# A graph layer's per-edge weights summed on GpSimd relation by relation, and VectorE's drain moved inside a pass

## The reference, cut to what matters

```python
N, IN, OUT, R, E = (2500, 768, 768, 8, 40000)   # called with 1250 nodes and 41250 edges, sorted by dst

def _rgcn_conv(x, src, dst, etype, W, root, b):
    seg = dst * num_rel + etype
    sums = jax.ops.segment_sum(x[src], seg, num_segments=num_nodes * num_rel)
    cnt = jax.ops.segment_sum(jnp.ones((src.shape[0],)), seg, num_segments=num_nodes * num_rel)
    mean = (sums / jnp.maximum(cnt, 1.0)[:, None]).reshape(num_nodes, num_rel, -1)
    return jnp.einsum('nri,rio->no', mean, W) + x @ root + b

h = relu(_rgcn_conv(xn, src, dst, etype, W1, root1, b1))
out = _rgcn_conv(h, src, dst, etype, W2, root2, b2)
```

## Time and profile before

| | |
|---|---|
| time, median of 3 | 3421.99 us (3419.77 to 3424.31) |
| the profiled execution | 3421.39 us, of it the span 3419.5 us |
| PE busy | 3174.5 us, 93% of the span |
| DVE busy | 1773.6 us, 52% |
| POOL busy | 1273.2 us, 37% |
| chain that ended last | PE 71%, DVE 12%, issue 7%, DVE's sequencer 6% |

### The profile page before, as it was taken

How to read it: one execution, slowest core, us unless ns; L and a number is a source line. 1 busy time by engine, 2 the same in 40 slices (tenths; PEclk the granted TensorE clock), 3 DMA queues, 4 the chain that set the end, 5 groups by cost and what they waited for, 6 DMA issues and landing times.

```text
span 3419.5 us, 64810 instructions
## 1 busy us (share of the span) xinstructions
PE 3174.5 (93%) x19556; PEld 2359.9 (69%) x19557; DVE 1773.6 (52%) x2941; ACT 762.8 (22%) x1086; POOL 1273.2 (37%) x1377
## 2 busy tenths in 40 slices
PE   6999999999997999999899989999886999999999
PEld 5788888777776888888677766776654555555555
DVE  7576666555555333333555552334586456455551
ACT  2211121000001212211000004444212543543540
POOL 2681000577772000002777761000420632652562
PEclk9999999999999999999999999999998999999999
DMA  5334334599994232321898882000330000000003
GB/s 149 101 106 149 118 116 137 171 306 307 306 306 140 87 120 94 118 95 63 319 307 307 303 287 78 14 28 14 88 95 24 20 1 19 19 1 19 19 28 95
DMA packets 101141, 433.58 MB, mean 127 GB/s; under 512 B 19648, under 2 KB 19971, under 8 KB 96818
## 3 DMA queue, kind: packets, MB, share of 16 engines
q0 software_dynamic: 55712, 266.87, 23.2%
q1 hardware_dynamic: 42593, 124.83, 11.6%
q10 hardware_dynamic: 2736, 40.50, 3.4%
HBM read 355.21 MB, written 76.88 MB: 126 GB/s over the span
## 4 chain that ended last, share of the span: by engine, by line
PE 71%; DVE 12%; issue 7%; DVEq 6%; ACT 1%; POOL 1%; DMA 1%; POOLq 0%; SPq 0%; ACTq 0%
PE PS L1466 26%; PE PS L1580 13%; PE PS L1776 5%; PE PS L1604 3%; PE PS L1711 3%; PE PS L1475 3%; DVE NM L1387 2%; PE PS L1612 2%; PE PS L1759 2%; PE PS L1760 2%; PE PS L1715 2%; PE PS L1649 2%; DVE HOT L1166 2%; PE PS L1633 2%; PE PS L1623 1%
## 5 line engine op out<-in xcount | busy, mean ns | idle before, releaser
L1466 PE MATMUL PS<-WHL,XT 128*125 (+1 forms) x3240 | 549.4, 329 | 7.0 <-DVE WHL L940 4.2
L1466 PE MATMUL PS<-WHL,HT 128*125 (+1 forms) x3240 | 531.8, 327 | 0.0
L1580 PE MATMUL PS<-GATA,HOT 128*125 128x384 f16 x2880 | 492.6, 328 | 37.0 <-issue 17.8
L1466 PEld LDWEIGHTS PS<-WHL,XT 128*125 (+1 forms) x3240 | 441.3, 138 | 92.7 <-issue 5.3
L1466 PEld LDWEIGHTS PS<-WHL,HT 128*125 (+1 forms) x3240 | 441.9, 137 | 84.2
L558 POOL DMA_INDIRECT GATA<-msg_table,SKEY x432 | 421.8, 976 | 163.0 <-issue 124.6
L1580 PEld LDWEIGHTS PS<-GATA,HOT 128*125 x2880 | 386.3, 137 | 114.5 <-issue 44.6
L1166 DVE SCALAR_TENSOR_TENSOR HOT<-NODE,DSTF,WHLO x720 | 297.0, 475 | 277.6 <-issue 277.6
L594 POOL TENSOR_TENSOR PL<-PF 125x500 bf16<-125x500 f32 (+1 forms) x360 | 320.6, 924 | 281.0 <-ACT PF L797 277.8
L1016 DVE SCALAR_TENSOR_TENSOR MSG<-PS,MSG 125x768 f16<-125x768 f32 x160 | 153.1, 957 | 360.3 <-ACT MSG L627 358.9
L627 ACT ACTIVATE MSG<-PS 125x768 f16<-125x768 f32 x160 | 129.6, 810 | 786.8 <-PE PS L1466 773.9
(11 more groups left out here) (254 smaller groups left out, 3898.6 us busy)
## 6 DMA issues: line engine op xcount, KB each, us to landing
msg_table<-MSG SPq DMA_DIRECT2D x160, 336.0 KB
WST<-in_wg_dram ACTq DMA_DIRECT2D x16, 2304.0 KB, 10.1
WST<-in_wf_dram SPq DMA_DIRECT2D x7, 1536.0 KB, 6.3
KROW<-key_rows POOLq DMA_DIRECT2D x54, 192.0 KB, 3.8
GATA<-msg_table,SKEY POOLq DMA_INDIRECT x432, 4.5
msg_table<-MSG SPq DMA_DIRECT2D x160, 39.0 KB
WST<-in_wm_dram SPq DMA_DIRECT2D x5, 1152.0 KB, 5.1
GATB<-msg_table,SKEY POOLq DMA_INDIRECT x216, 4.5
```

The lines of the kernel that those rows point to most:

```text
L1466: ins = pe.matmul(PS[0:ROWS, b0 + h, 0:HALF], X[:, xp, k, bass.ts(t, ROWS)], panel_part(slot, wp, k, h), start=k == 0 and xp + wp == 0, st ...
L1580: ins = pe.matmul(PS[0:ROWS, bass.ds(((n + (L + 1)) % 2) * 2 + h, 1), 0:HALF].rearrange("p a c -> p (a c)"), HOT[:, bass.ds((n % 2) * AT + ...
```

## The change

The weights are summed one relation at a time, as `GW` gets each column (`relation_in`), between GpSimd's key rows in layer 0 and before the gathers in layer 1, without the common factor, which `common_weight` multiplies in when all eight are known. In layer 0 the first four gathers are issued ahead of `edge_weights`, which now holds only the inverse counts and the split. In the passes the drain goes from ahead of the one-hots to the start of `take_pass`, which the final addition of a layer also calls.

```diff
+            def relation_weight(L, r):
+                g.wait_ge(S["relation_in"], L * REL + r + 1)
+                g.sem_inc(S["pool_tick"], 1)
+                if r == 0:
+                    g.tensor_scalar(WSUM[:], ETF[:, 0:TILES], 0.0, GW[:, 0:1], ALU.is_equal, ALU.mult)
+                else:
+                    g.tensor_scalar(TMPF[:], ETF[:, 0:TILES], float(r), GW[:, r:r + 1], ALU.is_equal, ALU.mult)
+                    g.drain()
+                    g.tensor_tensor(WSUM[:], WSUM[:], TMPF[:], ALU.add)
+                g.drain()
+            def common_weight(L):
                 g.wait_ge(S["relations_made"], L + 1)
                 g.sem_inc(S["pool_tick"], 1)
-                g.tensor_scalar(WSUM[:], ETF[:, 0:TILES], 0.0, GW[:, REL:REL + 1], ALU.is_equal, ALU.mult)
-                for r in range(1, REL):
-                    ... (mask times column, drain, add, drain)
+                g.tensor_scalar(WSUM[:], WSUM[:], GS[:, 1:2], None, ALU.mult)
+                g.drain()
+            def edge_weights(L):
                 (inverse counts, split, weights_made: as before)
+            for u in range(SLOTS):
+                (wait keys_made, send KROW: as before)
+                if u % RT == RT - 1:
+                    p = COUNTED + u // RT
+                    for r in range(0 if p == COUNTED else p, p + 1):
+                        relation_weight(0, r)
             for L in range(2):
-                edge_weights(L)
+                if L == 1:
+                    for r in range(REL):
+                        relation_weight(1, r)
+                common_weight(L)
+                if L == 1:
+                    edge_weights(1)
                 g.wait_ge(S["msg_out"], ROW_IN * REL * RT * (L + 1))
                 for t in range(TILES):
+                    if L == 0 and t == AT:
+                        edge_weights(0)
...
-                    v.tensor_copy(GW[:, bass.ds(p, 1)], SC[:, WINV])
+                    v.tensor_copy(GW[:, bass.ds(p, 1)], SC[:, WINV]).then_inc(S["relation_in"], 1)
...
-                    v.tensor_scalar(GW[:, REL:2 * REL], GW[:, 0:REL], GS[:, 1:2], W_TOP, ALU.mult, ALU.mult)
+                    v.tensor_scalar(GS[:, 1:2], GS[:, 1:2], W_TOP, None, ALU.mult)
...
                 def take_pass(n):
+                    v.drain()
                     v.wait_ge(S["pass_done"], n + (L + 2))
...
                         n = v.snap(cnt, min_val=0, max_val=1 << 20)
-                        v.drain()
                         v.wait_ge(S["pass_done"], n + (L + 1))
```

More of the change, by code:

```diff
@@ L148, in graph_and_attentions_kernel @@
         WHLO = sb(gctx, "WHLO", [128, TILES, 2], f16)
-        GW = sb(gctx, "GW", [128, 2 * REL], f32)
+        GW = sb(gctx, "GW", [128, REL], f32)
         GS = sb(gctx, "GS", [128, 3], f32)
@@ L213, in graph_and_attentions_kernel @@
             edges_in zeros_made bounds_made bounds_t lim_made
-            hot1_made hot1_used cnt_done hir_made hir_out key_in0 key_in1 key_in2 key_in3 key_in4 keys_ready low_made relations_made inverse_made rows2_in keys_made counts_found counts_taken
+            hot1_made hot1_used cnt_done hir_made hir_out key_in0 key_in1 key_in2 key_in3 key_in4 keys_ready low_made relations_made relation_in inverse_made rows2_in keys_made counts_found counts_taken
             hot_made gat_in0 gat_in1 gat_in2 gat_in3 gat_in4 gat_in5 gat_in6 gat_in7 gat_in8 gat_in9 gat_in10 gat_in11 pass_done pass_out group_used weights_made msg_hi rows_done
@@ L540, in edge_weights @@
                 g.sem_inc(S["weights_made"], 1)
-            for L in range(2):
-                edge_weights(L)
+            g.wait_ge(S["hir_out"], 16)
+            for u in range(SLOTS):
+                if u >= KRING:
+                    g.wait_ge(S["keys_made"], u - KRING + 1)
+                    g.sem_inc(S["pool_tick"], 1)
+                g.dma_start(KROW[:, u % KRING, :], key_rows[u:u + 1, :].broadcast_to([128, SLOT * 128])).then_inc(S[f"key_in{u % KRING}"], 16)
+                if u % RT == RT - 1:
+                    p = COUNTED + u // RT
+                    for r in range(0 if p == COUNTED else p, p + 1):
+                        relation_weight(0, r)
+            for L in range(2):
+                if L == 1:
[4 more added lines that the diff above has]
+                    edge_weights(1)
                 g.wait_ge(S["msg_out"], ROW_IN * REL * RT * (L + 1))
```

## The result

The changed kernel takes 3427.03 us (median of 20 runs, 3423.47 to 3430.99), the kernel before 3420.14 (20 runs, 3409.53 to 3429.01): a ratio of 1.0019 [1.0013, 1.0026], 6.9 us or 0.19% slower. The forecast was slower, 3434 us. The direction holds and the time lies in the range, but the size is half of what was forecast: 3434 us is 13.9 above the 3420.14 of these 20 runs. The profiled execution of after took 3427.76 us, its span is 3425.9 us; that is 6.4 us over the profiled one of before.

The account below looks back on a forecast made before the run. GpSimd's gathers were taken to bound both layers' passes before, VectorE layer 0 afterwards. 3421.4 + 10.7 (layer 0) + 1 (layer 1) = 3433.1, with the median 0.6 above the profiled execution: 3434 us, range 3424 to 3446.

Parts of the forecast that it names:

- weights and front gathers at nothing: Panels and ring start: GpSimd's waits of 24.72 us (layer 0) and 27.53 us (layer 1) cover the moved work, 0 us.
- The price for the ports: Key comparisons beside GpSimd's sums: 0.47 us for each of five stretches, 2.4 us at worst, taken as 0.
- the sequencer stands until the one-hots are done: VectorE's passes: with the moved drain it stands 1.65 us from the first one-hot, then needs 0.16 us to the wait.
- no change: Rival: the moved drain costs less than worked out and gathers still bound both layers; 3422 to 3424 us, chance 0.15.
- +10.7: Layer 0's passes: bound by VectorE at 4.86 us a group, 8.19 a double group, TensorE's last pass 10.7 us later.
- - 0.05: VectorE's turn in layer 0: removing the old drain's slot saves 0.05 us, giving 4.86 us a group with one pass.
- GpSimd wait about 11 us for the passes: Layer 0: gathers wait for L1586 behind double groups by several us in all, about 11.
- +1: Layer 1's passes: they catch up only just before the next double group and hold the ring longer, 1 us.
- They still set the end: Layer 1: gathers allow 2042.78, VectorE's pace would give 2039.3, 3.5 us earlier, so gathers remain the bound.
- both layers bound by VectorE: Rival: VectorE sets the pace in both layers, +10.7 + 9.4 us, 3442 us, chance 0.22.
- Faster: Rival: second one-hots of 18 double groups no longer wait for an addition, 0.5 us each, 9 us, 3413, chance 0.05.

Follow-up runs that it names:

- weights in PSUM: Kernel before with edge weights copied to PSUM for the one-hots and the drain moved into `take_pass`: 3420.76 us against 3420.91; with the old drain, 1.0018 to 1.0035.
- halved gathers: Kernel before with half of the gathers left out behind the first twelve: 3381.23 us with the old drain, 3422.87 with it moved into `take_pass`, against 3420.91.

## Why the prediction came out as it did

**Right: weights and front gathers at nothing.** The cover was there: the thirteenth gather waited 29.53 us and stayed within 0.4 us of its place, and the weights alone made no difference in three runs, all in the slower condition. The price for the ports, taken as 0, was 0: the key comparison's maximum is 436 ns now, where the earlier trace rows had 886.

**Right: the sequencer stands until the one-hots are done.** The drain's median is 856 ns (forecast 0.7 to 0.9), and from the one-hots to the wait it is 870.00 to 871.81, the forecast's 1.65 + 0.16. The rival "no change" is out. The Trainium skill's rule weighed there ("VectorE: DVE Perf Modes", section "The DRAIN you can't avoid") is on when the next operation starts. That a drain written as an instruction is therefore free was the prediction's reading of it, and this trace doesn't agree: it moved the sequencer's wait from 0.92 to 1.81 us behind the one-hots' start.

**Layer 0, a term mis-sized: +7.25 instead of +10.7.** The step is "- 0.05" for the old drain's slot in the 4.86 us. A turn is 1.65 + 0.16 + 3.10 - 0.11 = 4.80, and 4.82 was measured; a double group took 8.12 instead of 8.19. Over the 78 groups from the third pass that is 406.1 us (660.43 to 1066.54) instead of 409.0. The other 0.5 us is the start. The slot was read as the distance of the rows of its neighbours, and what the neighbours themselves lose by the instruction between them was not in it. Two drains against one showed 0.11. The forecast also had GpSimd wait about 11 us for the passes; its idle time grew by 2.8 us, and longer gathers filled 4.3.

**Layer 1, the step that failed: -3.1 instead of +1.** The step is "They still set the end": the time from the fifth gather to the last, 414.1 us or 1.298 a gather, was taken as GpSimd's own and fixed, and VectorE's pace, 3.5 us faster by the forecast's sum, as hidden behind it. In the runs VectorE's pace is 4.65 us a turn (forecast 4.68), the 0.11 again, and by that pace alone the passes take 412.3 to 413.0 us (weights in PSUM, halved gathers), 5.4 to 6.1 less than before. Of this the changed kernel got 3.1. Most of the rest is lost at block borders: at five of nine the turn behind the pair takes 5.1 to 5.6 us instead of the 4.9 with halved gathers. TensorE begins the pair late there, 1.2 to 1.6 us behind the first one-hot instead of 1.0 to 1.1; in the three cases whose landing the trace has, that is 2.9 to 3.4 us after the last gather of the group before landed. So the gathers still delay the layer there, and VectorE sets its pace nearly everywhere else.

The gathers didn't hold the layer at 418.4 us because their pace wasn't theirs alone: a gather that begins while one-hots run is longer. Behind the first 24 of layer 1, 60 took over 1.0 us before and 39 after; the mean of all 320 fell by 10 ns, 3.2 us in sum. Without any long gather, weights in PSUM, the mean is 945 ns and the same passes take 412.3 us. Why fewer gathers were hit in layer 1, and as many as before but for longer in layer 0 (62 and 64), was not tested; the turn of 4.65 us against one gather's 1.25 shifts the two against each other otherwise than a turn tied to four gathers does, and this is argued, not shown.

**By luck** the total looks nearer than its terms. The passes came out 7.5 us below their forecast, and the two stretches outside them, which the forecast had at nothing, gave back 2.3 us that belong to the spread.

The forecast weighed the sharing of SBUF's ports for the panels, where it was worth 0, and not for the passes, where it is worth more: 320 gathers of 978 instead of 945 ns is 10.6 us a layer, of which 6 to 7 came back with the one-hots by tensor_scalar, where VectorE has the old drain. The Trainium skill ("SBUF — State Buffer", section "SBUF: two separate sides") has a rule for it: a VectorE instruction with two inputs in SBUF and a GpSimd operation that reads SBUF exclude each other. The traces agree as far as durations go: up to 1.23 us beside such one-hots, and 0.94 to 0.96 when one input is in PSUM. Which port or lock it is, no run shows.

**Of the rivals**, "both layers bound by VectorE" had the mechanism nearly right and a wrong time, 3442: it added layer 1's cost with layer 0's turns. "Faster" had no visible part in the result.

**Open.** In the slower condition the kernel with the moved drain alone is 9 to 14 us faster than before in four series, and with both drains 3 to 13 us slower; taking the old drain out is worth 12 to 27 us there. 180 passes at 0.11 us are 20 us, and the second one-hots of a double group no longer wait for an addition; neither was isolated. The stretched sets differ too: over both layers they lose 45 to 59 us with the moved drain alone and 52 to 62 with both, against 73 to 80 where only the drain ahead of the one-hots stands and the weights are at their new place. Whether that is a cause isn't shown, nor what the holes are. Nor was the drain alone run where the kernel before takes 3421 us: that it makes layer 0's 7 us rests on the halved gathers and on the weights in PSUM, both with the old weights' place, 421.6 and 420.9 us against 422.5.

## What to carry to other kernels

A drain written into a loop costs by what its sequencer could have done meanwhile, so put it where the sequencer is late anyway; price it by removing one, not from its row. Before an engine's pace is taken as a floor, look whether its single instructions have two lengths and what runs beside the long ones: here the floor moved when VectorE's order moved, and another form of the one-hots, longer on VectorE, made the kernel 0.5% faster. Where two engines' paces lie close, the same edit can lengthen one stage and shorten its twin, so each stage needs its own sum for both engines, with the nearer one's slack in the range. And look for holes between instructions that wait for nothing before a low DMA rate is taken as the cause of a slow run.

## What the runs showed of the hardware

- A gather's instruction on GpSimd takes 0.945 us by itself and up to 1.23 when it begins while VectorE's one-hots with two SBUF operands run; behind the first 24 of a layer, with one operand in PSUM at most 0.96 and with the one-tensor form 1.02.
- A drain with nothing left to wait for took 0.11 us of VectorE's sequence (3.11 against 3.00 us), with a row of 19 ns.
- The same kernel before took 3420 us in two series and 3640 to 3644 in four, once of each kind on one chip. The 14 traces of the slower kind have 230 to 252 GB/s instead of 290 to 313 in the passes with all gathers, a granted clock of 0.90 to 0.96 instead of 0.99 to 1.00, DMA engines busy for 0.71 to 0.77 instead of 0.86 to 0.90, and holes of 10 to 45 us a layer between one-hots that wait for nothing. The moved drain alone is 0.2 to 0.4% faster there; it was not run in the quicker condition, where the whole change is 0.19% slower.
